# Output biases of two attentions added inside matrix products instead of by GpSimd, in a two-layer transformer kernel on one core

## What is computed

```
x = x + L0_xattn(ctx, layernorm(x), mask)   # 4 heads of 64; keys: x's own 1024 rows and 77 of the context
x = x + L0_ffn(layernorm(x))                # 1024 hidden, GELU, with a small input-dependent part
x = x + L1_xattn(layernorm(x), ctx)         # 8 heads of 64; keys: the 77 rows of the context
x = x + L1_ffn(layernorm(x))                # 8 experts, each takes 257 rows of either batch entry
# the end of either attention:
attn = softmax(scores); out = attn @ v      # per head
return out @ Wo + bo                        # bo: 256 numbers, the same for every row
# the end of the first FFN: ... + b2
```

## Time and profile before

| | us |
|---|---|
| median of 3 runs | 927.6 |
| lowest and highest | 918.29, 931.03 |
| profiled execution | 927.48 |
| its span in the trace | 925.7 |

### The profile page before, as it was taken

One profiled execution on the slowest core, in us unless ns is written; L12 is line 12 of the kernel. 1 busy time (PEld: TensorE's weight loads), 2 busy tenths in 40 slices (PEclk: granted clock), 3 DMA queues, 4 the chain that ended last, 5 costly groups with the idle time before them and its releaser, 6 DMA issues.

```text
span 925.7 us, 12588 instructions
## 1 busy us (share of the span) xinstructions
PE 785.5 (85%) x4720; PEld 628.3 (68%) x4720; DVE 556.4 (60%) x1140; ACT 394.9 (43%) x713; POOL 364.2 (39%) x308
## 2 busy tenths in 40 slices
PE   2648988989999999996999978688317999999996
PEld 2536554755555555576979967688316998999996
DVE  5766686566577485255433458787673666656642
ACT  2323543445445334462171233333304655665662
POOL 5533212320040013034352124332423787888883
PEclk9958999999999999998799869799657999999999
DMA  6000000000000010010002020111121323554432
GB/s 181 1 0 1 1 1 1 1 1 1 1 1 1 1 48 1 1 46 2 1 0 88 1 91 2 46 47 57 35 91 41 113 77 92 138 137 126 127 42 28
DMA packets 20394, 38.64 MB, mean 42 GB/s; under 512 B 4537, under 2 KB 15917, under 8 KB 18029
## 3 DMA queue, kind: packets, MB, share of 16 engines
q1 hardware_dynamic: 13677, 29.40, 9.3%
q0 software_dynamic: 6656, 8.43, 5.1%
HBM read 29.28 MB, written 8.40 MB: 41 GB/s over the span
## 4 chain that ended last, share of the span: by engine, by line
PE 62%; DVE 22%; issue 6%; ACT 6%; POOL 3%; DMA 1%; another core or an unknown queue 0%; SPq 0%; ACTq 0%; DVEq 0%; POOLq 0%
PE ps L436 20%; PE ps L1047 9%; PE ps L575 9%; PE ps L675 5%; DVE mx L1214 4%; PE ps L539 3%; PE ps L592 3%; PE ps L593 2%; DVE qkn L1173 2%; PE ps L516 2%; DVE rep L1604 1%; PE ps L996 1%; ACT htmp L1911 1%; PE ps L984 1%; POOL rs L2179 1%
## 5 line engine op out<-in xcount | busy, mean ns | idle before, releaser
L575 PE MATMUL ps<-PT,VA 128*65 128x512 f32 (+1 forms) x288 | 148.1, 596 | 0.2 <-ACT PT L1853 0.2
L1853 ACT ACTIVATE PT<-ps 128x512 f32<-128x512 f32 x128 | 76.0, 594 | 67.6 <-PE ps L593 67.0
L1214 DVE TENSOR_REDUCE mx<-ps 128x1 f32<-128x1104 f32 x64 | 83.5, 1304 | 34.9 <-PE ps L539 34.7
L1047 PE MATMUL ps<-he,wh 128*128 128x258 f32 x768 | 104.0, 288 | 0.0
L436 PE MATMUL ps<-GT,wh 128*128 128x258 f32 x768 | 98.3, 288 | 1.1 <-DVE GT L1693 1.1
L436 PEld LDWEIGHTS ps<-GT,wh 128*128 128x128 f32 x768 | 95.1, 192 | 1.5 <-issue 1.5
L1047 PEld LDWEIGHTS ps<-he,wh 128*128 128x128 f32 x768 | 95.3, 189 | 0.4
L2188 POOL TENSOR_TENSOR ssq<-ssq,half 128x4 f32<-128x4 f32 x32 | 32.4, 1012 | 127.2 <-DVE ssq L1155 126.9
L2179 POOL TENSOR_TENSOR rs<-rs,half 128x4 f32<-128x4 f32 (+2 forms) x19 | 17.8, 937 | 158.1 <-DVE rs L1087 151.1
L1723 DVE TENSOR_TENSOR he<-het,he 128x516 fp32r<-128x516 f32 x64 | 44.7, 698 | 58.0 <-ACT he L1747 44.0
L2451 POOL DMA_INDIRECT out_dram<-ye,idx x40 | 62.6, 1564 | 24.2 <-DVE ye L1705 14.3
(11 more groups left out here) (257 smaller groups left out, 1581.4 us busy)
## 6 DMA issues: line engine op xcount, KB each, us to landing
wr<-in_w1e_dram SPq DMA_DIRECT2D x8, 1024.0 KB
wr<-in_w2e_dram SPq DMA_DIRECT2D x8, 1024.0 KB
x<-in_x_dram SPq DMA_DIRECT2D x4, 512.0 KB, 7.6
w<-in_w_dram SPq DMA_DIRECT2D x2, 1024.0 KB, 4.7
y_dram<-yr SPq DMA_DIRECT2D x3, 512.0 KB, 3.0
out_dram<-x SPq DMA_DIRECT2D x3, 512.0 KB, 4.1
gt<-y_dram,idx POOLq DMA_INDIRECT x40
out_dram<-ye,idx POOLq DMA_INDIRECT x40
```

The costliest lines, as they stand in the source:

```text
L575: pe.matmul(bank[6 + hf][0:65, :], VA[b][0:K, kt, h, :], PT[u % 4][0:K, :], start=kt == 0, stop=kt == 8).then_inc(p_pv, 1)
L1047: op = pe.matmul(bank[dc][:, 0:258], w2h[i][:, wc_], he[j][:, m, 258 * c:258 * c + 258], start=n == 0, stop=n == 23)
L1214: v.tensor_reduce(mx[:, hi % 2, qt:qt + 1], ps[:, 0:3, 0:368], AX.XY, ALU.max).then_inc(v_mx, 1)
L1853: a.activation(PT[u % 4][0:K, :], bank[4 + u % 2][0:K, :], ACT.Exp, bias=0.0 if K == 128 else mcol[:, b:b + 1]).then_inc(a_exp, 1)
```

## The change

In layer 0 the bias goes into row 64 of wo_in for head 0 (zeros there for the other heads). That row is multiplied by the sum of the exponentials, and the result is divided by the same sum. In layer 1, `one`, one row of 128 numbers with 77 ones and then zeros, is multiplied by the row of bo and summed into the block of VW that holds head 0: the shares of head 0 sum to one. Eight of GpSimd's additions go, with their waits. wo_in is no longer in qkn but where the OT tiles are; so the split of wo may come later, and it does: ScalarE's copy between the preparation of head 1 and the first head, GpSimd's subtraction after the last of `scale_qk(0, 1)`; the first writing of OT[0] waits for it. The first half of qkn waits for two splits and no longer for three. Three tiles (row2, row1, one) replace rows.

```
--- before.py
+++ after.py
@@ -113,7 +113,9 @@
         stats = R0("stats", [128, NT, 6])
         mv = R0("mv", [128, NT, 2])
         rs = R0("rs", [128, NT])
-        rows = R0("rows", [128, 3, D])
+        row2 = R0("row2", [128, D])
+        row1 = R0("row1", [1, D])
+        one = R0("one", [1, 128])
         yb = [R0(f"yb{i}", [128, 4, D]) for i in range(2)]
         tsp = [R0(f"tsp{i}", [128, 512]) for i in range(2)]
         lng = R0("lng", [128, 2])
@@ -156,13 +158,15 @@
         mx = RA("mx", [128, 2, 8])
         mrt = [[RA(f"mrt{i}{j}", [4, 128], F32R) for j in range(2)] for i in range(2)]
         PT = [RA(f"PT{i}", [128, 512]) for i in range(4)]
+        ot_at = RA.at
         OT = [RA(f"OT{j}", [65, S], F32R) for j in range(2)]
+
+        wo_in = Arena(ot_at)("wo_in", [65, H0, 258])[:, :, :]
         rec = RA("rec", [128, 8])
 
         qkf = qkn[:, :, :, :, :].rearrange("p t h a d -> p (t h a d)")
         wqk_in = qkf[:, 0:1024].rearrange("p (k n) -> p k n", k=2)
         wv_in = qkf[:, 1024:1536].rearrange("p (k n) -> p k n", k=2)
-        wo_in = qkf[0:65, 1536:1536 + 1032].rearrange("p (k n) -> p k n", k=H0)
 
 
         s2 = Arena(R0.at)
@@ -285,6 +289,7 @@
         d_scat = sem("d_scat")
 
         g_init = sem("g_init")
+        g_one = sem("g_one")
         g_st = sem("g_st")
         g_rstd = sem("g_rstd")
         g_row = sem("g_row")
@@ -463,7 +468,7 @@
                 yield
                 pe.wait_ge(a_cT, b + 1)
                 if b == 0:
-                    pe.wait_ge(d_w, 144)
+                    pe.wait_ge(d_w, 160)
                 pe.matmul(bank[m][0:SC, :], ctxT[:, 0, 0:SC], wc[:, 0, :], start=True, stop=False)
                 pe.matmul(bank[m][0:SC, :], ctxT[0:64, 1, 0:SC], wc[0:64, 1, :], start=False, stop=True).then_inc(p_kv, 1)
                 busy[m] = (v_kcn, b + 1)
@@ -720,6 +725,8 @@
                     clear(m)
                     if b == 0:
                         pe.wait_ge(v_kd, 2)
+                        pe.wait_ge(d_rows, 32)
+                        pe.wait_ge(g_one, 2)
                     for q in range(4):
                         mc = slice(128 * q, 128 * q + 128)
                         pe.matmul(bank[m][:, 80 * q:80 * q + SC], wkv[:, 0, 1, mc], cT[:, 0, b, 0:SC], start=True, stop=False)
@@ -739,7 +746,10 @@
                             for q in qs:
                                 op = pe.matmul(bank[m][0:M, 256 * (c - c0):256 * (c - c0) + 256],
                                                VD[:, 616 * q + 128 * c:616 * q + 128 * c + M], wo1[:, q, :],
-                                               start=q == qs[0], stop=q == qs[-1])
+                                               start=q == qs[0], stop=q == qs[-1] and c > 0)
+                            if c == 0:
+
+                                op = pe.matmul(bank[m][:, 0:256], one[:, :], row1[:, :], start=False, stop=True)
                         op.then_inc(p_vw, 1)
                         busy[m] = (v_vw, 3 * b + j + 1)
                         yield
@@ -1166,8 +1176,8 @@
                     v.wait_ge(g_rq, 8 * P + 4 * gi + 4)
                     if gi == 0:
                         if P == 0:
-                            v.wait_ge(a_whi, 3)
-                            v.wait_ge(g_wlo, 3)
+                            v.wait_ge(a_whi, 2)
+                            v.wait_ge(g_wlo, 2)
                         else:
                             v.wait_ge(p_ht, 8 * P)
                     v.tensor_tensor(qkn[:, 4 * gi:4 * gi + 4, :, :, :].rearrange("p t h a d -> p (t h) a d")[:, :, 0, :],
@@ -1218,8 +1228,6 @@
                 v.wait_ge(p_wo, 8 * hi + qt + 1)
                 step(v.reciprocal(rec[:, qt:qt + 1], bank[m][:, 256:257]))
                 settle()
-                if hi % 4 == 0 and qt == 0:
-                    v.wait_ge(g_row, 2 * b + 2)
                 xs = x[:, 8 * b + qt, :]
                 v.scalar_tensor_tensor(xs, bank[m][:, 0:256], rec[:, qt:qt + 1], xs, ALU.mult, ALU.add).then_inc(v_x, 1)
 
@@ -1340,7 +1348,7 @@
                     xs = x[:, 4 * g + t, :]
                     v.wait_ge(p_y, 4 * g + t + 1)
                     if t == 0:
-                        v.wait_ge(g_row, 4 + g + 1)
+                        v.wait_ge(g_row, g + 1)
                     v.tensor_tensor(xs, bank[banks[t % 2]][:, 0:256], xs, ALU.add).then_inc(v_y, 1)
                     yield
 
@@ -1421,7 +1429,7 @@
             def product(n):
                 v.wait_ge(p_pv, 144 + n + 1)
                 if n % 4 == 0:
-                    v.wait_ge(g_row, 8 + n // 4 + 1)
+                    v.wait_ge(a_z, n // 4 + 1)
                 v.tensor_tensor(x[:, n, :], bank[1 + n % 2][:, 0:256], x[:, n, :], ALU.add).then_inc(v_x1, 1)
                 v.wait_ge(v_x1, n + 1)
                 step(v.bn_stats(stats[:, n, :], x[:, n, :]))
@@ -1517,7 +1525,7 @@
             first = ln(0)
             for _ in range(12):
                 next(first)
-            v.wait_ge(d_w, 144)
+            v.wait_ge(d_w, 160)
             v.scalar_tensor_tensor(gg[:, 2:3], gg[:, 0:1], DH ** -0.5, gg[:, 1:2], ALU.mult, ALU.mult)
             step(v.tensor_copy(mcol[:, :], mcol8[:, :]))
             settle()
@@ -1842,6 +1850,8 @@
                     a.wait_ge(p_pv, 18 * hi + 9 * hf + 9)
                     if hi:
                         a.wait_ge(p_wo, 8 * (hi - 1) + 4 * hf + 4)
+                    elif hf == 0:
+                        a.wait_ge(g_wlo, 3)
                     copy(OT[0][:, qc], bank[6 + hf][0:65, :]).then_inc(a_ot, 1)
 
                 for u in range(18):
@@ -2033,9 +2043,6 @@
             copy(wv[0], wv_in).then_inc(a_whi, 1)
             for _ in range(5):
                 next(first)
-            a.wait_ge(g_wo, 1)
-            a.wait_ge(d_w, 144)
-            copy(wo[0], wo_in).then_inc(a_whi, 1)
             p_, h_, c_ = proj(0, 0, lambda n: 2 + n % 4, True), head(0, 0, lambda n: 6 + n % 2), ctx(0, 0)
             for i in range(8):
                 next(p_)
@@ -2057,6 +2064,9 @@
             drain(h_)
 
 
+            a.wait_ge(g_wo, 1)
+            a.wait_ge(d_w, 160)
+            copy(wo[0], wo_in).then_inc(a_whi, 1)
             beside = [spaced(proj(0, 1, side, False), head(0, 2, side)), spaced(head(0, 3, side), ln(1, side), ctx(1, 3)),
                       spaced(proj(1, 0, side, True), head(1, 0, side)), spaced(head(1, 1, side)),
                       spaced(proj(1, 1, side, False), head(1, 2, side)), spaced(head(1, 3, side)),
@@ -2178,9 +2188,9 @@
                 g_.wait_ge(v_var, NORM[k])
                 g_.tensor_tensor(rs[0:P, n0:n0 + n], rs[0:P, n0:n0 + n], half[0:P, 0:n], ALU.pow).then_inc(g_rstd, 1)
 
-            def add_row(i, g):
+            def add_row(g):
                 g_.tensor_tensor(x[:, 4 * g:4 * g + 4, :], x[:, 4 * g:4 * g + 4, :],
-                                 rows[:, i:i + 1, :].to_broadcast([128, 4, D]), ALU.add).then_inc(g_row, 1)
+                                 row2[:, :].unsqueeze(1).to_broadcast([128, 4, D]), ALU.add).then_inc(g_row, 1)
 
             def root_q(P, i):
                 c = slice(4 * (i % 4), 4 * (i % 4) + 4)
@@ -2192,8 +2202,8 @@
                 g_.wait_ge(a_sq, 8 * P + 4 * gi + 4)
                 if gi == 0:
                     if P == 0:
-                        g_.wait_ge(a_whi, 3)
-                        g_.wait_ge(g_wlo, 3)
+                        g_.wait_ge(a_whi, 2)
+                        g_.wait_ge(g_wlo, 2)
                     else:
                         g_.wait_ge(p_ht, 8 * P)
                 g_.tensor_tensor(qkn[:, 4 * gi:4 * gi + 4, :, :, :].rearrange("p t h a d -> p (t h) a d")[:, :, 1, :],
@@ -2219,7 +2229,7 @@
             def lnf(g):
                 factors(("lnf", g), 4 * g, 4)
                 g_.wait_ge(v_z, 4 + g + 1)
-                add_row(1, g)
+                add_row(g)
 
             def w1_lora(b):
                 for n in range(4):
@@ -2251,10 +2261,6 @@
             def norm_n(g):
                 yield from idle(2)
                 factors(("n", g), 4 * g, 4)
-                yield
-                yield
-                g_.wait_ge(a_z, g + 1)
-                add_row(2, g)
                 yield
 
             def normed(n):
@@ -2333,6 +2339,10 @@
                         g_.indirect_dma_start(gt[ex % 2][0:M, s, :], None, y_dram,
                                               bass.IndirectOffsetOnAxis(ap=idx[0:M, ex, s:s + 1], axis=0)).then_inc(d_gat[ex % 2][c], 16)
 
+            g_.memset(one[:, SC:128], 0.0).then_inc(g_one, 1)
+            g_.wait_ge(g_one, 1)
+            g_.memset(one[:, 0:SC], 1.0).then_inc(g_one, 1)
+            g_.wait_ge(g_one, 2)
             g_.memset(ident[:, :], 0.0).then_inc(g_init, 1)
             g_.wait_ge(g_init, 1)
             g_.affine_select(out=ident[:, :], in_=ident[:, :], compare_op=ALU.not_equal, fill=1.0, base=0, pattern=[[-1, 128]],
@@ -2352,12 +2362,10 @@
             factors(("ln", 1), 4, 4)
             step(g_.memset(wo_in[:, :, 256:258], 0.0))
```

(20 more changed lines are left out.)

52 lines of the change are left out of this document (21 added, 31 removed).

## The result

The changed kernel takes 911.5 us (median of 17 runs, 909.3 to 918.9) against 923.0 for the kernel before on the same chip (17 runs, 918.3 to 931.0): a ratio of 0.9895, 95% interval 0.9874 to 0.9915. The forecast was 6.1 us less; it came to 11.5 less between the medians. Those 11.5 are the upper end of what can be said: the 17 runs of the changed kernel lie in two groups, nine from 909.3 to 911.5 and eight from 915.1 to 918.9, and the median is the last run of the lower group. The means (923.4 and 913.5) are 9.9 apart, and the ratio with its interval stands for 9.7 us, between 7.8 and 11.6. On another chip the same comparison gave 0.9877 (0.9829 to 0.9925), 920.3 against 930.4.

A forecast was written before the change was run, and what follows sets the result against it. TensorE, busy 85% of the span, bounds it, with GpSimd only 3% of the chain, so additions count only where they hold others up. Terms -0.24 -2.18 -1.1 -1.5 -1.8 +0.76 = -6.06 take 927.48 to 921.4 us; range 913 to 930.

The forecast's parts named there:

- C: Rival: clock stays up because the pause before 52.10 is 2.2 us shorter; -4.6 us, so 916.8; chance 0.10.
- memset of the start: GpSimd's memset beside VectorE's first normalizations shrinks from 1032 to 768 elements: 0.24 us off, between 0 and 0.8.
- first two additions: From 48.58, stretching VectorE's product for qkn, for which TensorE stood idle 7.92 us: gain 2.18 us.
- third and fourth: Additions at 134.36 and 13.4 us later, lying over a VectorE cast: gains 0.7 and 0.4, together between 0 and 1.5.
- layer 1, groups 0 and 1: Layer 1's additions for the first two groups, during the FFN's last tiles, hold up nothing: 0.
- 563.54: Layer 1 addition with the scaling of Pb queued behind it, TensorE idle 1.52 us: gain 1.5, between 0 and 2.4.
- 586.76: Layer 1 addition stretching VectorE's rs of the first route, TensorE idle 4.23 us: gain 1.8, between 0.8 and 2.4.
- one-row products: Two added TensorE products of 256 columns: 2 x 0.38 = 0.76 us lost, between 0 and 1.27.
- moved copy and split: ScalarE's copy before the first exponential, 0.26 us to spare, and GpSimd's split after it: 0 for both.
- A: Rival: cover of the moved copy and split fails, TensorE waits; price 3.5 us, so 924.9; chance 0.08.
- D: Rival: gains given back to TensorE's other waits, only qkn gain and added products left; 926.1; chance 0.12.
- one fall more: Rival B: the clock falls once more when a pause in the second attention meets such a fall; chance 0.12.

The follow-up runs named there:

- the pair of runs: Changed kernel with the first two additions put back, of zeros: 0.9933, 925.7 us; with ten GpSimd memsets there instead: one run, 926.1 us.
- the run with the old place: Changed kernel with wo_in in qkn again and ScalarE's copy and GpSimd's split back at the start: 0.9901 of the kernel before, 922.9 us.
- the run with fillers: Changed kernel with dummy TensorE products in the pauses of the first attention's start: 0.9896 of the kernel before, 921.2 us.
- either half of the change: Layer 0's bias change and moved split alone: 0.9952 of the kernel before, 927.4 us; layer 1's one-row products alone: 0.9965, 927.6 us.

## Why the prediction was right, and what it missed

**Right.** The way of reading: neither the share of GpSimd nor the sum of its additions (eight by 2.38 us is 19), but for each one what it lies over. Each place that was to gain gained, and the places said to be free were free. Within 2% was given 0.94, and every comparison of the whole change is within it. There is luck in the size: the ends of the terms gave 918.2 to 925.8, and 917.9 (0.9895 of the 927.6 from which the forecast started) lies inside the range only because that was widened for the spread of the runs and for C, which didn't come.

**Term by term** (forecast, measured in the profiled pair, from idle times or from how much earlier the same TensorE instruction starts than at the place before):

| term | forecast | measured | read from |
|---|---|---|---|
| memset of the start | -0.24 | -0.22 | idle before 20.93: 3.56, now 3.34 |
| first two additions | -2.18 | -2.04 | idle 7.92, now 5.88; 5.38 and 3.34 in the pair of runs |
| third and fourth | -0.7, -0.4 | -0.7, -0.74 | 1.80 earlier at 138.40 (from 1.15), 2.54 at 152.43 |
| layer 1, groups 0 and 1 | 0 | 0 | the run with these two put back |
| 563.54 | -1.5 | -1.7 | idle 1.52, now none; 1.7 with all put back |
| 586.76 | -1.8 | -0.9 | idle 4.23, now 3.37; 0.94 with all put back |
| one-row products | +0.76 | +1.64 | 2 x 0.82, the run without them |
| moved copy and split | 0 | 0 | 0.34 of cover left; the run with the old place |
| sum | -6.06 | -4.6 | |

The sum of the direct terms was 1.5 us too large, by two terms (the others came a little better): the one-row products cost 0.9 more (their price was that of a product of 128 rows), and the stretched rs of the first route was worth 0.9 and not 1.8. The rs did become 1.80 shorter (1.97 to 0.17), but TensorE's wait behind it fell by 0.86 only; what else ended that wait the trace doesn't name ("issue"). Of the rivals, A didn't come: 0.34 us of cover were left, for 0.26 read. D (gains given back) didn't either: the lead of 2.54 at 152 is still there, to 0.3, when the next stretch of different speed begins at 424. C: the clock of the first head fell in spite of the shorter pause, as the text said; what it would have been worth, 4.6, the run with fillers puts at 4.0.

**What the sum left out.** The direct terms are 4.6 us and the change is worth 9.7 (7.8 to 11.6), so some 5 us are in no term. The prediction treated the clock as two rivals, one fall more (0.12) and one fall less (-4.6, 0.10), each by itself, and put 0 in the sum. (One fall more is some 14 us, an estimate: three quarters of the 18.5 us of TensorE in slice 24 at half the clock. No run shows that fall, slice 24 is 9 after as before; with all additions put back the clock was 0.53 for 18 us and the lag grew by 4.7.) The runs show less lost to the clock with the change: before 66.6 us in the mean of 64 executions on three chips, after 60.6 in 22 on two. But that is not 6.0 us of time. Among the runs of one kernel, a us more of this loss goes with 0.36 to 0.43 us of time (before, three chips) or 0.56 (the changed kernel's first 17), and the run with fillers has 5.7 less of it and no gain; by these slopes 6.0 are an estimated 2.2 to 3.4 us. With the terms that makes 6.8 to 8.0, at the lower end of the interval. Nor is it shown that the shorter pauses are the cause: with either half of the change the loss was that of the kernel before, and with all additions put back it was above it (73.1 against 65.5). In the profiled pair, 16.2 us apart, 4.6 are terms, 4.2 stand in the experts' stage, and the other 7.4 are stretches in which the same instructions run at different speeds: 4.8 gained at 424 to 451, 1.5 at 513 to 517 and 1.2 at 540 to 547, 1.7 lost at 30 to 33 and 1.2 at 495 to 505, and the rest in smaller ones. These differ between records of one kernel as well.

**Open.** Why the changed kernel loses less to the clock, which of the additions that hangs on, and what the 2 to 3 us are that neither the terms nor the clock gives. Single records differ too much: of the changed kernel's own 17 runs the nine at 909.3 to 911.5 have a clock of 0.935 to 0.940, the eight at 915.1 to 918.9 have 0.924 to 0.932. And what the waits named "remote" are, which come and go between records of the same code.

## What to carry to other kernels

Price an elementwise instruction on GpSimd by what lies beside it on VectorE and who waits for that, not by its length: of 19 us of additions 6.0 were on the path, in five places, and two additions cost nothing. A small VectorE instruction in front of a transfer was a bad place here for GpSimd's addition, which reads SBUF and took 2.4 us (17 rows by 256: 2.47 beside it, 0.41 ahead of it); a wait that puts the addition behind it was worth 2.05 and 2.19 us at two places. Read what a stretched instruction costs at the engine that waits, not from its own length (1.80 shorter, 0.86 gained). Price a product from when the next one starts, with the instructions that it is made of. And where the clock of TensorE falls often, give the sum a range for it that is taken from several executions: one pair of profiles showed 16.2 us for a change that is worth some 10.

## What the runs showed of the hardware

GpSimd's own memsets, 5.77 us of them, left a VectorE product of two SBUF inputs alone (1.23 us), while additions that read and write SBUF stretched it to 3.27; VectorE's instruction of 17 rows by 256 was stretched from 0.41 to 2.47. A float32 product of 256 columns is two instructions in these traces, with one row of contraction (4 for 2 products) as with 128 (32 for 16); the one-row product took TensorE 0.82 us, those of 128 rows beside it some 0.4. TensorE's granted clock was 1.00 up to 50 us and 0.50 behind the pause of 5.88; with the fillers it was 1.00 from 58 on, without them 0.50 up to 74, 0.85 from 74 to 75 and 1.00 then. Less time at half clock was not as much time won: 0.36 to 0.43 us per us of loss among the runs of the kernel before, 0.56 among the first 17 of the changed kernel, and nothing with the fillers. And one kernel's executions on one chip lie 9.6 us apart (909.3 to 918.9), as far as the whole change moves them.
